# A selective-scan layer: one product of each step moves from VectorE to GpSimd, and the output chain keeps its intermediate in PSUM

## The reference

```python
xn = layernorm(x)
x_and_res = xn @ in_proj_w.T + in_proj_b
x_in = silu(x_and_res[..., :1024]);  res = x_and_res[..., 1024:]
ssm = x_in @ x_proj_w.T + x_proj_b
dlt_raw, Bm, Cm = ssm[..., :16], ssm[..., 16:1040], ssm[..., 1040:]
delta = clip(softplus(dlt_raw @ dt_proj_w.T + dt_proj_b), 1e-5, 0.1)
A = clip(-exp(A_log), -5.0, -0.01)                      # 1024 x 16
# for each time t, each channel, each of 16 states:
h = clip(h * clip(exp(A * dt), 1e-6, 1) + (B * dt * x)[..., None], -100, 100)
y = sum(h, axis=-1) * C + D_param * x
attn = (y * silu(res)) @ out_proj_w.T + out_proj_b
ffn = xn @ W.T + bias          # W unfolded from two small tensors
return x + attn + ffn
```

## Time and profile before

| | |
|---|---|
| time, median of 3 runs | 1364.24 us (1362.29 to 1365.52) |
| the profiled execution | 1363.85 us, its slowest core's span 1362.3 us |
| spans of the 8 cores | 1356.8 to 1362.3 us |
| granted TensorE clock, mean by core | 0.813 to 0.854 |
| scan (L734), 256 of them | 1119.5 us of VectorE, 4424 ns each |
| output chain (L750, L757, L770), 64 each | 43.6, 47.8 and 43.9 us |
| clip, t1, u (L753, L762, L775) | 18.1, 26.8 and 26.1 us |

### The profile page before, as it was taken

The page is one execution under the profiler, slowest core; times in us unless marked ns, Lnnn a source line. Parts: engine busy times, 40 slices in busy tenths (PEclk is TensorE's granted clock), DMA queues, the critical chain, the costliest instruction groups (busy, mean ns, idle before and its releaser), DMA issues.

```text
span 1362.3 us, 16727 instructions; the slowest of 8 cores (1356.8 to 1362.3 us)
## 1 busy us (share of the span) xinstructions
PE 1159.2 (85%) x4352; PEld 454.8 (33%) x4352; DVE 1329.3 (98%) x821; ACT 1190.7 (87%) x1899; POOL 72.0 (5%) x101
## 2 busy tenths in 40 slices
PE   5687886899888888799997898898888999878987
PEld 2232332333333333233333343333333333333432
DVE  6899999999999999999999999999999999999996
ACT  3899989989899898998989989899988988799781
POOL 1010100000000000000000000000000000110100
PEclk9886776878778898777778887788977888898877
DMA  9666855455654465444583555554554346454421
GB/s 278 100 110 98 126 99 141 108 109 89 117 117 72 109 124 98 104 111 86 117 127 72 102 116 126 80 108 92 106 101 90 54 78 139 82 147 85 93 50 63
DMA packets 94508, 143.97 MB, mean 106 GB/s; under 512 B 31232, under 2 KB 55360, under 8 KB 94416
## 3 DMA queue, kind: packets, MB, share of 16 engines
q1 hardware_dynamic: 80736, 117.99, 35.4%
q0 software_dynamic: 13680, 24.91, 17.4%
HBM read 101.45 MB, written 35.65 MB: 101 GB/s over the span
## 4 chain that ended last, share of the span: by engine, by line
PE 28%; DVE 28%; issue 21%; ACT 18%; DMA 4%; DVEq 1%; ACTq 0%; SPq 0%
DVE h L734 24%; ACT da L894 10%; PE pS L500 7%; PE pB L467 4%; DMA u<-u 3%; PE pC L477 3%; PE pX L435 2%; PE pO L435 2%; PE pR L487 2%; PE pO L514 2%; PE pO L511 2%; PE pX L511 2%; DVE y L750 1%; PE pX L514 1%; ACT L894 1%
## 5 line engine op out<-in xcount | busy, mean ns | idle before, releaser
L734 DVE TENSOR_TENSOR_SCAN h<-da,u 128x2056 f16<-128x2056 f16 x256 | 1119.5, 4424 | 3.4 <-ACT da L877 1.8
L894 ACT ACTIVATE da<-dl,consb 128x512 f16<-128x512 f16 x1024 | 651.7, 711 | 1.7 <-DVE dl L753 1.0
L500 PE MATMUL pS<-h,eye 128*128 128x512 f16 x1024 | 316.5, 442 | 160.3 <-DVE h L734 160.1
L500 PEld LDWEIGHTS pS<-h,eye 128*128 128x128 f16 x1024 | 102.2, 107 | 340.5 <-issue 316.0
L467 PE MATMUL pB<-xin,wx 128*128 128x512 f16 x512 | 167.9, 488 | 2.8 <-DMA wx<-w_x 2.2
L477 PE MATMUL pC<-xin,wx 128*128 128x512 f16 x512 | 140.8, 425 | 0.0
L487 PE MATMUL pR<-xnT,win 128*128 128x512 f16 x512 | 137.0, 417 | 0.0
L365 POOL DMA_DIRECT2D yt<-ost x56 | 47.8, 854 | 1049.1 <-ACT ost L955 1017.2
L467 PEld LDWEIGHTS pB<-xin,wx 128*128 128x128 f16 x512 | 54.3, 116 | 96.1 <-issue 87.2
L477 PEld LDWEIGHTS pC<-xin,wx 128*128 128x128 f16 x512 | 55.6, 109 | 79.1 <-issue 63.3
L894 ACT ACT_TABLE_LOAD x63 | 80.8, 1283 | 1.1
(11 more groups left out here) (140 smaller groups left out, 917.6 us busy)
## 6 DMA issues: line engine op xcount, KB each, us to landing
wo<-wos SPq DMA_DIRECT2D x56, 512.0 KB, 6.5
xt<-x SPq DMA_DIRECT2D x48, 512.0 KB, 5.9
u<-u SPq DMA_DIRECT2D x62, 384.0 KB, 3.2
yt<-xt SPq DMA_DIRECT2D x60, 256.0 KB, 7.8
yt<-ost POOLq DMA_DIRECT2D x56, 256.0 KB, 5.6
wx<-w_x POOLq DMA_DIRECT2D x15, 256.0 KB, 8.9
xnT<-x SPq DMA_DIRECT2D x4, 512.0 KB, 7.1
da<-w_in SPq DMA_DIRECT2D x4, 512.0 KB, 11.3
```

What stands on the lines that cost most here:

```text
L500: mm = te.matmul(pS[s % 2][:, :], eye[:, :], h[:, n * SEG + 2:(n + 1) * SEG], start=(n == 0), stop=(n == NST - 1))
L734: v.tensor_tensor_scan(h[:, g * GW:(g + 1) * GW], da[:, g * GW:(g + 1) * GW], u[p][:, :], 0.0, op0=ALU.mult, op1=ALU.add).then_inc(v_scan, 1)
L894: sc.activation(da[:, n * SEG + 2:(n + 1) * SEG], dl[s % 2][:, :], AF.Exp, scale=cc(C_AL + k * NST + n)).then_inc(act_da, 1)
```

## The change

VectorE's order is rewritten. The three instructions of the output chain stand together, in place on the PSUM bank of S; the tile y1 is gone. The clip of dl moves behind the fourth scan of the step before. t1 is computed on GpSimd (`dt_x`), which waits until the step's first scan is done; u waits for it. TensorE's waits on a PSUM bank of S go from the first product's semaphore to yb's, and ScalarE's wait before it overwrites dl goes to GpSimd's. Steps 0 and 1 keep the clip and t1 on VectorE.

```diff
@@ GpSimd
+            def dt_x(w):
+
+                c, k = divmod(w, DCH)
+                gp.wait_ge(v_cl, w + 1)
+                gp.wait_ge(v_u, w)
+                gp.wait_ge(v_scan, (w - 1) * NG + 1)
+                gp.tensor_tensor(t1[:, :], dl[w % 2][:, :], seg(xin[c % 2], k), op=ALU.mult).then_inc(g_t1, 1)
...
             for s in range(0, NSL):
+                if 2 <= s + 1 < NSL:
+                    dt_x(s + 1)
                 for (c, m) in out_at[s - 1]:
                     accumulate(c, m)
@@ TensorE
                 if g == 0 and s >= 2:
-                    te.wait_ge(v_SC, s - 1)
+                    te.wait_ge(v_y, s - 1)
...
-                        te.wait_ge(v_SC, NSL - 7 + m)
+                        te.wait_ge(v_y, NSL - 7 + m)
@@ VectorE
+            def clip_dl(w):
+                v.wait_ge(act_ln, w + 1)
+                v.tensor_scalar(dl[w % 2][:, :], dl[w % 2][:, :], 0.1, 1e-5,
+                                op0=ALU.min, op1=ALU.max).then_inc(v_cl, 1)
+
             for s in range(-1, NSL + 1):
                 if 0 <= s < NSL:
                     scan(s, 0)
-                if 0 <= s - 1 and keeps(s - 1):
-                    clip_carry(s - 1, 1, NG)
...
                 if 0 <= z < NSL:
                     v.wait_ge(pe_s, z * NG + NG)
                     v.wait_ge(act_C, z + 1)
-                    v.tensor_mul(y1[:, :], pS[z % 2][:, :], Cf[z % 2][:, :]).then_inc(v_SC, 1)
-                if w < NSL:
-                    v.wait_ge(act_ln, w + 1)
-                    v.tensor_scalar(dl[w % 2][:, :], dl[w % 2][:, :], 0.1, 1e-5,
-                                    op0=ALU.min, op1=ALU.max).then_inc(v_cl, 1)
-                if 0 <= z < NSL:
+                    v.tensor_mul(pS[z % 2][:, :], pS[z % 2][:, :], Cf[z % 2][:, :]).then_inc(v_SC, 1)
                     v.wait_ge(v_SC, z + 1)
-                    v.scalar_tensor_tensor(y1[:, :], seg(xin[c % 2], k), cc(C_D + k), y1[:, :],
+                    v.scalar_tensor_tensor(pS[z % 2][:, :], seg(xin[c % 2], k), cc(C_D + k), pS[z % 2][:, :],
                                            op0=ALU.mult, op1=ALU.add).then_inc(v_D, 1)
-                if w < NSL:
-                    cw, kw = divmod(w, DCH)
-                    v.wait_ge(v_cl, w + 1)
-                    v.tensor_mul(t1[:, :], dl[w % 2][:, :], seg(xin[cw % 2], kw)).then_inc(v_t1, 1)
-                if 0 <= z < NSL:
                     v.wait_ge(v_D, z + 1)
                     v.wait_ge(act_R, z + 1)
...
-                    v.tensor_mul(seg(yb[c % 2], k), y1[:, :], rs[z % 2][:, :]).then_inc(v_y, 1)
+                    v.tensor_mul(seg(yb[c % 2], k), pS[z % 2][:, :], rs[z % 2][:, :]).then_inc(v_y, 1)
+                if 0 <= s - 1 and keeps(s - 1):
+                    clip_carry(s - 1, 1, NG)
...
+                elif w < NSL:
+                    v.wait_ge(g_t1, w - 1)
+                    v.wait_ge(act_B, w + 1)
+                    v.tensor_mul(u[w % 2][:, 2:SEG], Bf[w % 2][:, :], t1[:, :]).then_inc(v_u, 1)
...
                     scan(s, 3)
+                    if s + 2 < NSL:
+                        clip_dl(s + 2)
@@ ScalarE
-                    if w >= 2:
+                    if w >= 4:
+                        sc.wait_ge(g_t1, w - 3)
+                    elif w >= 2:
                         sc.wait_ge(v_t1, w - 1)
                     sc.activation(dl[w % 2][:, :], pDT[:, :], AF.Ln, bias=1.0).then_inc(act_ln, 1)
```

More of the change, by code:

```diff
@@ L116, in build_core @@
         rs = [sb(f"rs{i}", [128, TC], F16) for i in range(2)]
-        y1 = sb("y1", [128, TC], F32)
         xt = [sb(f"xt{i}", [128, D], F32) for i in range(2)]
@@ L179, in build_core @@
         v_eye, v_ini, v_ac, v_bc = sem("v_eye"), sem("v_ini"), sem("v_ac"), sem("v_bc")
-        g_io = sem("g_io")
+        g_io, g_t1 = sem("g_io"), sem("g_t1")
         d_cons, d_g = sem("d_cons"), sem("d_g")
@@ L769, in _ @@
                         v.wait_ge(d_wff, 32)
-                    v.tensor_mul(seg(yb[c % 2], k), y1[:, :], rs[z % 2][:, :]).then_inc(v_y, 1)
-                if w < NSL:
+                    v.tensor_mul(seg(yb[c % 2], k), pS[z % 2][:, :], rs[z % 2][:, :]).then_inc(v_y, 1)
+                if 0 <= s - 1 and keeps(s - 1):
+                    clip_carry(s - 1, 1, NG)
+                if w < 2:
+                    clip_dl(w)
+                    v.wait_ge(v_cl, w + 1)
+                    v.tensor_mul(t1[:, :], dl[w][:, :], seg(xin[0], w)).then_inc(v_t1, 1)
                     v.wait_ge(v_t1, w + 1)
                     v.wait_ge(act_B, w + 1)
-                    if w >= 2:
[L775 to L779, removed]
+                    v.tensor_mul(bass.AP(u[w], 2, [[GW, 128], [SEG, GRP], [1, TC]]),
+                                 Bf[w][:, :].unsqueeze(1).broadcast_to([128, GRP, TC]),
+                                 t1[:, :].unsqueeze(1).broadcast_to([128, GRP, TC])).then_inc(v_u, 1)
+                elif w < NSL:
+                    v.wait_ge(g_t1, w - 1)
+                    v.wait_ge(act_B, w + 1)
+                    v.tensor_mul(u[w % 2][:, 2:SEG], Bf[w % 2][:, :], t1[:, :]).then_inc(v_u, 1)
                 if s == -1:
```

## The result

The changed kernel takes 1373.97 us (median of 4 runs, 1371.93 to 1375.37), the kernel before beside it 1364.86. The ratio is 1.0072, 95% interval 1.0061 to 1.0084: 8.3 to 11.5 us slower. The forecast was 1371.2. Measured a second time, the ratio was 1.0082 (1.0069 to 1.0095), 11.1 us.

The account below looks back on a forecast made before the run. VectorE was taken as the bound, busy 1329.3 of 1362.3 us. Steps 0.11 us longer (62 x 0.11 = 6.8) plus 0.5 for extra waits gave +7.3 on 1363.85, 1371.2 us; range 1361 to 1389, the forecast's own 1364 to 1379.

Parts of the forecast that it names:

- t1 leaves VectorE for 0.34 us a step, not its 0.42: VectorE's row: t1 lasts 0.42 us but takes only 0.34; 62 x 0.34 = 21.1 us taken off.
- The uncovered pairs: Output chain without clip and t1 between: first product to D term 0.79, D term to yb 0.92; 0.19 and 0.26 uncovered.
- The step, 0.11 us longer: VectorE's step: 0.34 us removed, 0.45 uncovered, so 0.11 longer; 62 x 0.11 = 6.8 us.
- The waits behind the blocking one: First step of chunks 1 to 7: yb's third semaphore wait costs 0.07 us more, 7 x 0.07 = 0.5 us.
- PSUM costs nothing: Output chain's intermediate in PSUM: no cost taken; bounds 0.06 us on two spacings, 7.4 us either way.
- GpSimd's product, 1.1 us: t1 on GpSimd: start up to 0.60, product 1.1, visible 0.1; 1.8 us, hidden with 0.5 to spare before u.
- GpSimd's queue: Output accumulations go out behind the next step's product, landing by 1298, before the evacuation at 1303.34: hidden.
- 1 (PSUM gives back 0.12 us): Output chain: PSUM results visible to VectorE 0.06 us sooner, twice a step; time 1364, chance 0.17.
- 2 (no latency): Output chain costs no latency, so the full 21 us is won: 1343 us, chance 0.08.
- 3: GpSimd's product arrives after u could start, 2.28 us after the scan; 1385 us with a 1.8 us product, chance 0.12.
- 4: VectorE's chain and GpSimd's product block each other over a shared SBUF path: 68 us, 1439 us, chance 0.10.

Follow-up runs that it names:

- the pipelined order: The changed kernel with yb of the step before computed between this step's first product and D term: 1344.62 us, 0.9857 of the kernel before.
- the kernel with PSUM alone: The kernel before with only y1 replaced by S's PSUM bank, order and t1 on VectorE kept: 1361.7 us against 1362.42, ratio 0.9994.
- the reordered kernel before: The kernel before, all on VectorE and y1 in SBUF, reordered to clip, first product, D term, yb, t1, u: 1407.03 us, ratio 1.0329.

## Why the prediction was right

The forecast gave +7.3 us, 1371.2, with a range from 1361 to 1389; measured were +9.1 between the medians (+11.1 the second time) and 1373.97, inside both its ranges. The mechanism is the one forecast, and its cost was put 2 to 4 us too low. Point by point:

- **t1 leaves VectorE for 0.34 us a step, not its 0.42.** Held: adding it to the pipelined order lengthens a step by 0.33.
- **The uncovered pairs.** Held in place and size: 0.77 and 0.93 against the 0.79 and 0.92 forecast from the program's end, and the order alone reproduces it without GpSimd or PSUM. The chain and the clip sum to 2.91 in the step shown, forecast 2.90.
- **The step, 0.11 us longer.** Somewhat low: 20.35 against 20.21 is 0.14, from spacings that are each 0.01 or so longer. Over 62 steps that is 8.7 us with the chunk starts where the forecast had 7.3, and the profiles of the kernel without the product and of the kernel with PSUM alone differ by just that (1263.39 and 1254.70 us from the first product of output 0 to that of output 62).
- **The waits behind the blocking one.** Held: in the seven steps that begin a chunk yb comes 0.24 us after the D term's end instead of 0.17. The 12.6 us of the wait row are 57 x 0.17 + 7 x 0.24 = 11.4, and three of the longer pairs, 1.1.
- **PSUM costs nothing.** Held: 0.78 and 0.93 in SBUF, 0.77 or 0.78 and 0.93 in PSUM; both bounds, 0.06 either way, were wider than the truth.
- **GpSimd's product, 1.1 us.** Measured 1.15. Its start was mis-sized: 0.14 to 0.17 us after the scan's end, not up to 0.60, which had been read from the start of a DMA issue. It is seen 0.18 after its end, not 0.1; the slack was 0.8 us, where I gave it 0.5.
- **GpSimd's queue.** Held. ScalarE's longest waits, in total, are for TensorE, none for the accumulations:

```profile
ACT ost L967 <- PE pO L523: 30.8, 11, 3.5
ACT Cf L933 <- PE pC L486: 26.5, 26, 2.1
ACT L856 <- PE pO L444: 14.5, 9, 2.0
```

- **What was not foreseen**: the eight gaps of 0.35 us, 2.8 us, of which the kernel before has one. With the 1.4 us of the step they come to 3.9 us, against 2 to 4 between forecast and results; the times are not exact enough to part the two.
- **Rivals.** 1 (PSUM gives back 0.12 us) is refuted by the spacings, which are the same in both memories; the kernel with PSUM alone could not show it, since nothing there waits for its neighbour. 2 (no latency) is refuted by the reordered kernel before. 3 needs a far longer product: the doubled one, over at 2.67 us, was late. 4 exists, but only for instructions that the change had kept away from the product.

The rule of the Trainium skill that was weighed (VectorE: DVE Perf Modes, "The DRAIN you can't avoid": a semaphore between chained operations costs nothing) would have given 1343 us as the prediction read it. It does not hold for these rows: 0.78 us where the neighbour is awaited, 0.60 where it is not. The same section adds that a next operation that is not held starts earlier, and with that the rows of the covered order agree (0.09 us before the reported end).

## What to carry to other kernels

On a bound engine, an instruction between a producer and its reader is not only work but cover: before taking one away, look for the same pair elsewhere in the trace without it, and count the difference of the starts (here 0.19 us with one wait in the reader's row, and 0.07 more for each further one) against what leaves. Moving work to GpSimd paid here once two things held: what runs beside it reads one tile from SBUF and is none of the fp16 instructions with one source (clip, carry), and the dependent chain that it was covering has another cover, such as a member of the previous step's chain. The same offload lost 0.7% with the chain uncovered and gained 1.3% with it covered.

## What the runs showed of the hardware

- A dependent VectorE instruction starts 0.10 us after its producer's reported end with one wait in the row, 0.17 with two and 0.24 with three; an independent one starts 0.09 before that end. It is the same for a result in SBUF and in PSUM.
- GpSimd begins its product 0.14 to 0.17 us after the scan that releases it ends, a fp16 product of two 512-column tiles takes it 1.15 us, the next one after a wait starts 0.14 after (723.85 to 723.99), and VectorE starts 0.18 after the end of a product that it waits for.
- Its product and a VectorE instruction with two SBUF inputs, or the fp16 clip or carry, hold each other up; in the kernels where they met, whoever came first went on at full speed (scan 4.43 us, product 1.15). The other's reported duration grows (5.08 us for a product behind a scan, 0.95 for a clip), so such contention is found in the mean durations, not in the waits.
- Open: why VectorE loses 0.35 us at eight fixed places of the changed kernel's program, at one of the kernel before, at one of the pipelined kernel and at none of the one without the product. The eight are the same in each profile of the changed kernel and in those of the kernels with y1 in SBUF, with the doubled product and with the product released early.
